# Taking GpSimd's hold operations out of a loop of indirect gathers and scatters, and waiting on the landed transfers instead

## The reference, cut to what matters

```
x = x + tanh(g_xattn) * attention(ctx, layernorm(x), b, lens)
# the mixture of experts: 8 experts, each row uses the best 2
gates = top_2_softmax(cos_scores + route_scores)
h = gelu(einsum('bsd,edh->bseh', xn, w1) + b1)        # 512 -> 256
expert_out = einsum('bseh,ehd->bsed', h, w2) + b2      # 256 -> 512
x = x + tanh(g_ffn) * einsum('bse,bsed->bsd', gates, expert_out)
```

## Time and profile before

| | |
|---|---|
| median of 3 runs | 2145.31 us (2139.34 to 2153.35) |
| profiled execution | 2141.61 us, span of its instructions 2139.6 us |
| mean granted TensorE clock | 0.955 |
| busy over the span | PE 89%, DVE 75%, ACT 53%, POOL 34% |
| steps of the block loop | 36, first `yout` at 1564.1 us, last at 2120.7 us |

### The profile page before, as it was taken

One profiled execution on the slowest core, in us unless ns is written; L12 is line 12 of the kernel. 1 busy time (PEld: TensorE's weight loads), 2 busy tenths in 40 slices (PEclk: granted clock), 3 DMA queues, 4 the chain that ended last, 5 costly groups with the idle time before them and its releaser, 6 DMA issues. The chain is left out here.

```text
span 2139.6 us, 38585 instructions
## 1 busy us (share of the span) xinstructions
PE 1901.1 (89%) x10720; PEld 1060.5 (50%) x10721; DVE 1597.0 (75%) x3742; ACT 1127.1 (53%) x1999; POOL 737.5 (34%) x547
## 2 busy tenths in 40 slices
PE   0599999999999999999999999998399988989887
PEld 0344444444444444444444444443277766767675
DVE  6578788777877878877777787773477777777776
ACT  0166655656556565655655665654155555555554
POOL 1112111111111111211201111100168888888887
PEclk9899999999999999998999999998599999999999
DMA  3878687676867877777777786653358677777674
GB/s 110 141 109 162 117 181 139 133 153 125 179 133 137 178 142 134 162 114 173 142 130 151 126 184 111 140 125 125 98 114 145 135 132 138 149 125 131 131 135 67
DMA packets 173114, 292.01 MB, mean 136 GB/s; under 512 B 37982, under 2 KB 42078, under 8 KB 172944
## 3 DMA queue, kind: packets, MB, share of 16 engines
q1 hardware_dynamic: 140016, 222.26, 51.0%
q0 software_dynamic: 32928, 67.68, 17.8%
HBM read 127.09 MB, written 71.63 MB: 93 GB/s over the span
## 5 line engine op out<-in xcount | busy, mean ns | idle before, releaser
L918 DVE TENSOR_REDUCE mx<-bank 128x1 f32<-128x512 f32 x1024 | 693.8, 687 | 243.6 <-PE bank L714 231.5
L622 ACT ACTIVATE prob<-bank 128x512 f32<-128x512 f32 x1024 | 579.6, 596 | 492.1 <-PE bank L702 491.4
L590 POOL TENSOR_TENSOR regrouped_then_w<-regrouped_then_w 128x512 fp32r<-128x512 f32 x128 | 166.5, 1301 | 1145.9 <-ACT regrouped_then_w L612 1145.9
L714 PE MATMUL bank<-stA,stB 98*128 98x512 f32 x1024 | 428.4, 420 | 67.4 <-DVE mx L918 40.8
L702 PE MATMUL bank<-stB,stA 100*128 100x512 f32 x1024 | 469.2, 460 | 9.8 <-issue 9.5
L702 PEld LDWEIGHTS bank<-stB,stA 100*128 100x128 f32 x1024 | 196.9, 193 | 212.5 <-ACT prob L622 116.3
L675 PE MATMUL bank<-prob,vin 128*32 128x512 f32 x2048 | 279.6, 619 | 0.0
L675 PE MATMUL bank<-prob,ones 128*32 128x512 f32 x2048 | 278.9, 617 | 0.0
L1150 POOL DMA_INDIRECT rows_in<-xn_rows,gather_ids x152 | 221.3, 1456 | 162.7 <-DVE rows_in L1360 121.3
L714 PEld LDWEIGHTS bank<-stA,stB 98*128 98x128 f32 x1024 | 202.8, 198 | 113.2 <-DVE mx L918 73.0
L1180 POOL DMA_INDIRECT out_dram<-yout,scatter_ids x144 | 231.7, 1609 | 39.2 <-issue 30.4
(11 more groups left out here) (182 smaller groups left out, 2095.6 us busy)
## 6 DMA issues: line engine op xcount, KB each, us to landing
stB<-regrouped_then_w SPq DMA_DIRECT2D x192, 256.0 KB, 5.5
stA<-regrouped_then_w SPq DMA_DIRECT2D x192, 256.0 KB, 8.4
x_k_then_w<-in_x_dram SPq DMA_DIRECT2D x16, 1024.0 KB, 6.1
x_k_then_w<-in_ctx_dram SPq DMA_DIRECT2D x16, 1024.0 KB, 8.6
vin<-in_ctx_dram SPq DMA_DIRECT2D x16, 1024.0 KB, 6.4
xres<-in_x_dram SPq DMA_DIRECT2D x16, 1024.0 KB, 12.8
xn_rows<-xn SPq DMA_DIRECT2D x64, 256.0 KB, 2.2
out_dram<-xres SPq DMA_DIRECT2D x16, 1024.0 KB, 10.5
```

The lines of the kernel that those rows point to most:

```text
L590: pool.tensor_tensor(turnedL[:, side, :], turned[:, side, :], turnedH[:, side, :].bitcast(F32), ALU.subtract).then_inc(s_lo, 1)
L622: act.activation(prob[:, u % 2, j, :], psS[j % 2][:, :], ACT.Exp).then_inc(s_exp, 1)
L714: pe.matmul(psM[s % 2][:, :], stB[0:98, g, j, i * P:(i + 1) * P], stA[0:98, g, j, :], start=True, stop=True).then_inc(s_m, 1)
L918: dve.tensor_reduce(mx[:, s // 4, s % 4:s % 4 + 1], psM[s % 2][:, :], AX.X, ALU.max).then_inc(s_mx, 1)
```

## The change

Both holds leave the loop. In their place stands `pool.sem_inc(f_go, 1)`, an instruction of the queue's sequencer alone that counts up a semaphore which nobody waits for. DVE's two waits for `f_hold` become waits for the landed scatters themselves (`f_add`): before it writes `yout` it waits for the scatters of two blocks ago, which used the same buffer; before it writes `scatter_ids` it waits for the scatters of the block before. The count is worked out by the new function `added`. So that both parities count alike, the dummy transfer at the start (`nowhere_d`) is issued twice, once for each semaphore. POOL's waits for the row numbers, the gates, the landed scatters of the block before, and `yout` stay.

```diff
-            f_hold = sem("pool_held")
+            f_go = sem("pool_goes_on")
...
-            adds = [(f_y, 2 * NS), (f_yg, 2 * NS), (f_yo, 2 * NS), (f_hold, 4)]
+            adds = [(f_y, 2 * NS), (f_yg, 2 * NS), (f_yo, 2 * NS)]
...
+            def added(st, back):
+
+                return st.rnd * (16 * NS) + (16 if back == 1 and st.h else 16 - 16 * NS)
...
-                    def carry_wait():
-                        pool.tensor_tensor(hold[:, 5:6], ones[:, 0:1], ones[:, 0:1], ALU.add).then_inc(f_hold, 1)
-
...
-                            pool.indirect_dma_start(nowhere_d, bass.IndirectOffsetOnAxis(ap=nowhere[:, 0:1], axis=0),
-                                                    nothing[:, :], None, bounds_check=P - 1,
-                                                    oob_is_err=False).then_inc(f_add[1], 16)
+                            for i in range(2):
+                                pool.indirect_dma_start(nowhere_d, bass.IndirectOffsetOnAxis(ap=nowhere[:, 0:1], axis=0),
+                                                        nothing[:, :], None, bounds_check=P - 1,
+                                                        oob_is_err=False).then_inc(f_add[i], 16)
                             return
                         h = st.h
 
-                        pool.wait_ge(f_hold, st.rnd * 4 + 2 * h)
                         pool.wait_ge(f_use, st.steps(USES, -1, 2 + USES))
                         pool.wait_ge(f_gate, st.steps(1, -1, 1))
-                        carry_wait()
+                        pool.sem_inc(f_go, 1)
                         gather(st.par(1))
 
 
-                        pool.wait_ge(f_hold, st.rnd * 4 + (2 * h + 1))
-
-                        pool.wait_ge(f_add[1 - h], st.rnd * (16 * NS) + (0 if h else 16 - 16 * NS))
+                        pool.wait_ge(f_add[1 - h], added(st, 1))
                         pool.wait_ge(f_yo, st.back(NS, 0, NS))
-                        carry_wait()
+                        pool.sem_inc(f_go, 1)
...
-                            dve.wait_ge(f_hold, st.rnd * 4 + 2 * st.h)
+                            dve.wait_ge(f_add[st.h], added(st, 2))
...
-                            dve.wait_ge(f_hold, st.rnd * 4 + (2 * st.h + 2))
+                            dve.wait_ge(f_add[1 - st.h], added(st, 1))
```

More of the change, by code:

```diff
@@ L1186, in _ @@
                     n = n_rounds(pool)
-                    pool.wait_ge(f_add[0], n * (16 * NS))
+                    pool.wait_ge(f_add[0], n * (16 * NS) + 16)
                     pool.wait_ge(f_add[1], n * (16 * NS) + 16)
```

## The result

The changed kernel takes 2126.8 us against 2144.2 us (medians of 20 executions each); the ratio is 0.9916, 95% interval 0.9896 to 0.9936. That is 17 to 18 us won, 0.84%. The forecast was 38 us; the time lies in the stated range, but at the place of the first rival (2129 us), and less than half of the forecast gain came. Of all executions in this study one, of e2's kernel, took 9807.7 us for a reason that isn't known; it is left out of that ratio.

What follows compares the result with a forecast made beforehand. POOL's queue was taken to bound the loop at 15.85 us a step. Falling to 14.8 us over 35 periods gives 36.8 us, plus 1.5 us at the end: 38.3 us won, 2107 us, range 2088 to 2132 us.

Steps and rivals of the forecast that it cites:

- the first rival: In POOL's queue the holds' wait passes into the gathers; 16 us won, 2129 us, chance 0.16.
- What bounds the kernel: In the block loop the chain of waits runs through POOL, with a period of 15.85 us a step.
- Point 1: Holds leave POOL's queue: its step falls from 15.85 to 14.76 us if transfers keep their mean durations.
- Point 2: DVE's wait at the row-number copy, 51.2 us, goes since scatters land in time; no second gain.
- Points 3 to 5: DVE's wait before `yout`, the counting and register instructions, and the second dummy transfer at the start: each taken as 0.
- Point 6: At the end, the last scatters can start some 1.5 us earlier behind the last `yout`.
- lower bound of 14.4 us a step: Fast end of the forecast's own range for the loop's period: 55 us won, 2090 us.
- PE's idle time for rows and its low clock behind it: In the loop, PE's wait falls well under 36 us, and few windows have a granted clock under 1.00.
- The rule on the shared interfaces: GpSimd contends with two-SBUF-input DVE instructions; the gather after the removed hold would win 0.35 us, not 1.33 us.
- The slower rival: Gathers without holds fall beside DVE's instructions, 1.75 us each; POOL's step 16.6 us, 2171 us, chance 0.09.

Runs made afterwards that it cites:

- e2: Changed kernel with only the hold behind the last gather put back, DVE waiting for it at both places: 2143.3 us, ratio 0.9990.
- e4: Changed kernel with `yout` reading one input from PSUM and one from SBUF, ACT scaling the bias instead: 2088.2 us, ratio 0.9755.
- e11: Changed kernel with only the hold ahead of the first gather put back, DVE waiting for landed scatters: ratio 0.9896.
- e12: The changed kernel run again unaltered, as partner of e11 in the same session: ratio 0.9901.
- e1: Kernel before with both holds kept, only DVE's two waits changed to the landed scatters: 2124.6 us, ratio 0.9913.
- e8: Changed kernel, without holds, with DVE's copy of row numbers also waiting until this step's gathers have landed: 2160.2 us, ratio 1.0086.
- e6: Changed kernel with DVE's loads of expert numbers and tile_steps moved behind the first two turned rows: 2139.8 us, ratio 0.9994.
- e9: Kernel of e4 with w2's low part on DVE moved behind the search for the next rows: 2086.7 us, ratio 0.9729.
- e10: Kernel of e7 with w2's low part on DVE moved behind the search for the next rows: 2068.6 us, ratio 0.9648.
- e7: Changed kernel with the edits of e4 and e6 together: 2080.1 us, ratio 0.9723.

## Why the prediction was wrong

- *What bounds the kernel* was right for the kernel before, whose chain of waits runs through POOL. In the changed kernel POOL's queue is still full (15.46 of 15.53 us), and relieving it (e4) takes the ratio from 0.9916 to 0.9755, but the chain runs mostly elsewhere.
- *Point 1, the failing step:* "POOL's step falls from 15.85 us to 14.76 us if the transfers keep their mean durations". They did not. Gathers rose by 0.084 us and scatters by 0.091 us in the mean, 0.70 us a step, where the sum had 0. The premise that the hold-ups "come from DVE and not from the holds" was true and pointed the other way: a hold is a POOL operation that DVE holds up, so when it goes, the next POOL operation is held up in its place. e2 shows it for hold A (gathers 1.665 us, no gain), e11 against e12 too. For hold B the scatters beside w2's low part show it (2.09 us); no run takes hold B out while DVE's copy waits as before.
- *Point 2* had the mechanism of the wait right (it vanished, and the landed scatters were in time), but said that it "isn't a second gain on top of point 1". In fact it is the only gain that the runs can tell: e1 gives 0.87% with both holds in, and e8 takes more than all of it back without a hold. The sum should have had this term, about 0.5 us a step (15.85 to 15.35 us in e1), in place of the 1.05 us of point 1.
- *Points 3 to 5* at nothing: no run takes them apart, and nothing in the traces speaks against them (`yout` has no row for a wait on scatters). *Point 6*, 1.5 us at the end, doesn't show: from the last `yout` to the end of the span it is 2139.6 - 2120.7 = 18.9 us before and 2120.4 - 2100.2 = 20.2 us after. By the prediction's own sum its lower bound of 14.4 us a step is worth 35 x 1.45 + 1.5 = 52 us, and not 55 us; that changes nothing here.
- *PE's idle time for rows and its low clock behind it* were expected to go; they stayed (38.0 and 31.5 us against 36.5 us, and 0.72 of the clock behind a pause), and some gathers are still late.
- *The rule on the shared interfaces* deserved more than a chance of 0.16. The prediction read the delay right from rows (0.92 us behind w1's low part, measured 0.95 us) and then didn't put it into the sum. e4 confirms the rule for this kernel: with one SBUF input `yout` holds up no gather, at the same length. The Trainium skill ("GPSIMD Engine Reference", Key points) names DVE instructions with two SBUF inputs as contending; the trace agrees: 2.98 us against 1.04 us. But not every gather beside such an instruction is held up (1.00 us at 1772.10 us).
- *The first rival's time* (2129 us, measured 2126.8 us) was met by luck. It was added up from 0.35 us won at hold A and 0.1 us at hold B. Yet e2, without hold A, wins nothing, and e1, with both holds, wins it all.
- *The slower rival* had the right mechanism with the wrong frequency; e6 is the case in which it happens (gather mean 1.68 us of the 1.75 us from which it decides, no gain left).

**Open:** why DVE's wait at the copy matters while POOL's queue stays full. What the traces show is that POOL's time for a step is its plain 13.0 us (an estimate of the prediction, from gathers that nothing holds up) and the hold-ups by DVE, that these depend on where DVE's instructions fall (e6), and that with DVE free they are smaller (0.48 us a step in e1). One delay feeds the next in the traces: a gather that starts within 0.04 us of `yout` is held up where the gather ahead of it was, and not otherwise (last section). That DVE's wait at the copy makes such series more frequent fits all this, but no run shows it by itself.

## What to carry to other kernels

A short operation of one engine that seems to cost 1 us may be waiting for something that the next operation will wait for as well: look at what it ends with, and price its removal by what the next one does at that place. Where two chains are nearly equal and hold each other up, changes don't add: pair them and measure the pair (e9 gave nothing that can be told over e4, e10 gave 0.75% over e7). Before taking an operation out of a full queue, look for the reason that the queue's other operations are long; here one input moved from SBUF to PSUM was worth 1.6% on top of the change, about twice the change itself (0.9755 against 0.9916, both beside the kernel before).

## What the runs showed of the hardware that I had not expected

- An indirect gather on POOL can be held up by DVE's instructions with two SBUF inputs, for as long as they follow one another closely: 2.98 us beside four of 0.74 us, 4.78 us in e6, against 1.00 to 1.08 us alone. The same four with one input in PSUM: 1.04 us.
- The same start doesn't always give the same hold-up. The gather below starts with `yout`, as that at 1708.37 us does, and takes 1.00 us and not 2.98. What goes with it is the gather ahead. In the trace of the changed kernel 21 gathers start within 0.04 us of the first `yout` of a step. The 18 whose forerunner was itself held up (1.29 us or more) take 2.97 to 2.98 us, and the three whose forerunner took 1.04 or 1.08 us take 1.00 to 1.04 us. In the kernel before it is five of 2.96 to 2.97 us and four of 1.04 to 1.05 us, divided in the same way, and the other traces with two SBUF inputs have no exception. At 0.06 us it no longer divides them so (2.92 us at 1816.76 us, behind a gather of 1.08 us), and why the forerunner matters isn't known.

```profile
1770.75 1.04 POOL L1151 DMA_INDIRECT rows_in<-xn_rows,gather_ids  x1 [0.31 <-issue]
...
1772.08 2.75 DVE L1338 SCALAR_TENSOR_TENSOR yout<-b2s,row_gates,out_gated_rows 128x512 f32<-128x512 f32 x4
1772.10 1.00 POOL L1151 DMA_INDIRECT rows_in<-xn_rows,gather_ids  x1 [0.31 <-issue]
```

- A part of the kernel that was not touched, ahead of the loop, took 1551 to 1572 us in the traces of this study, a spread as large as the whole effect.
